# A graph network on one core: where the rows of the first attention layer are multiplied

## The reference

```python
def sage_layer(h, Ws, Wn, b):                      # network 1, three times
    agg = jax.ops.segment_sum(h[src], dst, num_segments=N) / deg
    return jax.nn.relu(h @ Ws + agg @ Wn + b)

def gat_conv(x, src, dst, W, att_src, att_dst, bias, heads, C, concat):   # network 2, twice
    h = (x @ W).reshape(n, heads, C)
    a_src = jnp.einsum('nhc,hc->nh', h, att_src)
    a_dst = jnp.einsum('nhc,hc->nh', h, att_dst)
    e = jax.nn.leaky_relu(a_src[src] + a_dst[dst], NEG_SLOPE)
    ...                                            # softmax of e over the edges of one dst: alpha
    out = jax.ops.segment_sum(h[src] * alpha[:, :, None], dst, num_segments=n)
    return out.reshape(n, heads * C) + bias
```

## Time and profile before

| | |
|---|---|
| time, median of 3 runs | 7210.41 us (7204.28 to 7210.7) |
| profiled execution, its own time | 7209.73 us |
| its span | 7207.8 us, mean PE clock 0.801 of full |
| PE busy | 5032.8 us (70%) |
| DVE busy | 4784.7 us (66%) |
| ACT busy | 3062.6 us (42%) |
| POOL busy | 3388.1 us (47%) |
| DMA | 1317.61 MB, mean 183 GB/s |

### The profile page before, as it was taken

One profiled execution on the slowest core, in us unless ns is written; L12 is line 12 of the kernel. 1 busy time (PEld: TensorE's weight loads), 2 busy tenths in 40 slices (PEclk: granted clock), 3 DMA queues, 4 the chain that ended last, 5 costly groups with the idle time before them and its releaser, 6 DMA issues. The chain is left out here.

```text
span 7207.8 us, 88239 instructions
## 1 busy us (share of the span) xinstructions
PE 5032.8 (70%) x24324; PEld 3367.5 (47%) x24324; DVE 4784.7 (66%) x14503; ACT 3062.6 (42%) x6979; POOL 3388.1 (47%) x3407
## 2 busy tenths in 40 slices
PE   7999995798989920697435555444489998679221
PEld 5777771364558810596323232221156665456111
DVE  5888789733347612888885566677878886655454
ACT  4666660263333300654444444336756554346000
POOL 5666000274434454373567666673300001765677
PEclk9999999999998955597557667665589999889555
DMA  5888551496766621696445698757856665766332
GB/s 194 277 276 277 214 198 61 126 305 226 245 205 203 195 67 35 175 350 212 140 137 148 129 136 131 122 100 219 270 197 222 222 223 199 209 203 194 95 93 82
DMA packets 1093011, 1317.61 MB, mean 183 GB/s; under 512 B 110351, under 2 KB 791999, under 8 KB 1086254
## 3 DMA queue, kind: packets, MB, share of 16 engines
q1 hardware_dynamic: 974926, 1058.13, 44.3%
q0 software_dynamic: 117600, 253.84, 17.3%
HBM read 633.42 MB, written 682.00 MB: 183 GB/s over the span
## 5 line engine op out<-in xcount | busy, mean ns | idle before, releaser
L615 POOL DMA_INDIRECT jk_layer_msg<-jk,idx_jk x588 | 591.5, 1006 | 268.2 <-issue 174.0
L615 POOL DMA_INDIRECT gcn_msg<-x,idx x196 | 186.9, 954 | 898.0 <-POOLq L137 838.6
L1148 PE MATMUL jk_layer_sum_ps<-ident,jk_layer_weighted 128*128 128x128 f32 x784 | 185.5, 380 | 540.5 <-ACT jk_layer_weighted L1114 540.5
L1148 PEld LDWEIGHTS jk_layer_sum_ps<-ident,jk_layer_weighted 128*128 128x128 f32 x784 | 118.6, 188 | 660.2 <-ACT jk_layer_weighted L1114 660.2
L742 PE MATMUL gcn_nodes_h_ps<-gcn_nodes_h_t,w_gcn 128*128 128x512 f32 x784 | 352.7, 593 | 0.0
L742 PE MATMUL sage_nodes_h_ps<-sage_nodes_h_t,w_ws 128*128 128x512 f32 x784 | 352.5, 592 | 0.0
L1282 DVE COPY sage_h<-sage_turn 128x512 f32<-128x512 f32 x98 | 67.7, 691 | 417.3 <-PE sage_turn L733 417.3
L615 POOL DMA_INDIRECT sage_small_rows<-meta,src_node x196 | 185.0, 944 | 324.2 <-POOLq L137 264.8
L962 ACT ACTIVATE sage_nodes_h_t<-sage_nodes_h_ps,w_b_c 128x512 f32<-128x512 f32 x392 | 247.8, 683 | 198.8 <-PE sage_nodes_h_ps L742 198.8
L2185 PE MATMUL gcn_end_sum_ps<-ident,gcn_end_rows 128*128 128x128 f32 x196 | 54.6, 434 | 389.4 <-DVE gcn_end_rows L2178 389.4
L615 POOL DMA_INDIRECT sage_end_msg<-h,idx x196 | 197.0, 1005 | 270.2 <-ACT sage_end_weighted L1114 159.5
(11 more groups left out here) (481 smaller groups left out, 15979.2 us busy)
## 6 DMA issues: line engine op xcount, KB each, us to landing
h<-sage_nodes_h SPq DMA_DIRECT2D x196, 512.0 KB
h_t<-sage_h_t SPq DMA_DIRECT2D x98, 512.0 KB
h<-sage_h SPq DMA_DIRECT2D x98, 512.0 KB, 3.6
jk_t<-jk_layer_h_t SPq DMA_DIRECT2D x196, 256.0 KB
jk_end_layers<-jk_t SPq DMA_DIRECT2D x49, 1024.0 KB, 5.3
r<-gcn_nodes_h SPq DMA_DIRECT2D x98, 512.0 KB
second_x_in<-u SPq DMA_DIRECT2D x147, 260.0 KB
jk<-jk_layer_h SPq DMA_DIRECT2D x147, 256.0 KB, 4.5
```

The costliest lines, as they stand in the source:

```text
L615: pool.indirect_dma_start(out=into[:, g.number % depth, s, :], out_offset=None, in_=table, in_offset=bass.IndirectOffsetOnAxis(ap=index_ti ...
L1148: mm = pe.transpose(ps[:, c, at_s], self.weighted[:, g.b, s, c * P:(c + 1) * P], self.K.ident[:])
```

## The change

The product of the first attention layer moves. For slots it was made at the end of `sage_end_block` and stored, and the fetch gathered its rows. Now `sage_end_block` ends with the norm and stores x1 only, and the fetch is replaced by `products_block("products1")`, the former second product made general: per round it takes one group of edges, whose rows of **x1** POOL gathers, and one group of slots, whose rows of x1 SP loads, and turns, copies and multiplies both. Edge results go to `kept`, slot results to `u`, scores beside them. For edges whose source is a node without edges, x1 must be in memory too, so `node_net_block` stores it: one more store of 256 KB per group on SP's queue, placed between the stores of h2 and u, and one more wait of DVE. In `sage_end_block` the own rows and the inputs get three buffers and the product two banks, and the product takes the own rows first. Nobody gathers scores any more, so `u` has 128 columns instead of 130 everywhere, and `attend_block` and the second product use rows of 512 bytes. The second product is otherwise the same code under new names.

```diff
-        x1_t, u = ph.sb("x1_t", [P, 2, 1, GROUP]), ph.sb("u", [P, 2, SUB, D + 2])
+        x1_t, u = ph.sb("x1_t", [P, 2, 1, GROUP]), ph.sb("u", rows4)
         x2 = ph.sb("x2", rows4)
         x1_turned, x1_copied, u_made, u_out, z_summed = (S(n) for n in ("x1_turned", "x1_copied", "u_made", "u_out", "z_summed"))
-        u_stored = ph.dma_sems("u_stored")
+        u_stored, x1_stored = ph.dma_sems("u_stored"), ph.dma_sems("x1_stored")
...
+        def store_x1(g):
+            wait_for(sp, norm.done, g)
+            sp.dma_start(at(node_rows(tables["x1"], SLOTS), g), z[:, g.b]).then_inc(x1_stored.of(g), 16)
+
         def store_u(g):
             wait_for(sp, u_biased, g)
             sp.dma_start(at(node_rows(tables["u"], SLOTS), g), u[:, g.b]).then_inc(u_stored.of(g), 16)
         if sage:
-            stages = [(load, -1), (reload, 3), (store_h1, 3), (store_h2, 4), (store_u, 7), (store_y, 6)]
+            stages = [(load, -1), (reload, 3), (store_h1, 3), (store_h2, 4), (store_x1, 5), (store_u, 7), (store_y, 6)]
         else:
             stages = [(load, -1), (reload, 4), (store_x3, 2), (store_h1, 4), (store_h2, 5), (store_y, 6)]
         run_groups(sp, NG, stages)
-        for stored in (h1_stored, h2_stored, y_stored) + ((u_stored,) if sage else (x3_stored,)):
+        for stored in (h1_stored, h2_stored, y_stored) + ((u_stored, x1_stored) if sage else (x3_stored,)):
...
-            layer_rows(pe, ring[:, :, 0:D + 2], [(W.wide["gat1"][:, :, 0:D + 2], x1_t[:, g.b])]).then_inc(u_made.sem, 1)
+            layer_rows(pe, ring[:, :, 0:D], [(W.m["gat1"], x1_t[:, g.b])]).then_inc(u_made.sem, 1)
...
                 wait_for(dve, x1_turned, g.lag(2))
+                wait_for(dve, x1_stored, g.lag(2))
...
-    own_t, own_ready = ph.sb("own_t", [P, 2, 2, GROUP]), A_("own_ready")
-    x1_t, u = ph.sb("x1_t", [P, 2, 1, GROUP]), ph.sb("u", [P, 2, SUB, D + 4])
-    x1_ps, u_ps = ph.ps("x1_ps", [P, GROUP]), ph.ps("u_ps", [P, SUB, HID])
-    x1_turned, x1_copied, u_made, u_out, att_out = (S(n) for n in ("x1_turned", "x1_copied", "u_made", "u_out", "att_out"))
-    u_stored = A_("u_stored")
-    x_in, y, z = (ph.sb(n, rows4) for n in ("x_in", "y", "z"))
-    y_ps = ph.ps("y_ps", [P, GROUP])
+    own_t, own_ready = ph.sb("own_t", [P, 3, 2, GROUP]), A_("own_ready", 1, 3)
+    x_in, y, z = ph.sb("x_in", [P, 3, SUB, D]), ph.sb("y", rows4), ph.sb("z", rows4)
+    y_ps = [ph.ps(f"y_ps{b}", [P, GROUP]) for b in range(2)]
     norm = Norm(ph, "norm")
-    x_loaded, z_stored = A_("x_loaded"), A_("z_stored")
+    x_loaded, z_stored = A_("x_loaded", 1, 3), A_("z_stored")
     made, biased, added = S("made"), S("biased"), S("added")
     block = ph.block()
 
     @block.sync
     def _(sp):
         def load_own(g):
-            wait_for(sp, made, g.lag(2))
-            sp.dma_start(own_t[:, g.b], at(tables["h2_t"], g)).then_inc(own_ready.of(g), 16)
+            wait_for(sp, made, g.lag(3))
+            sp.dma_start(own_t[:, g.number % 3], at(tables["h2_t"], g)).then_inc(own_ready.of(g), 16)
 
         def load_x(g):
-            wait_for(sp, added, g.lag(2))
-            sp.dma_start(x_in[:, g.b], at(slot_rows(tables["x_own"]), g)).then_inc(x_loaded.of(g), 16)
+            wait_for(sp, added, g.lag(3))
+            sp.dma_start(x_in[:, g.number % 3], at(slot_rows(tables["x_own"]), g)).then_inc(x_loaded.of(g), 16)
 
         def store_x1(g):
             wait_for(sp, norm.done, g)
             sp.dma_start(at(slot_rows(tables["x1"]), g), z[:, g.b]).then_inc(z_stored.of(g), 16)
-
-        def store_u(g):
-            wait_for(sp, u_out, g)
-            sp.dma_start(at(slot_rows(tables["u"]), g), u[:, g.b, :, 0:D + 2]).then_inc(u_stored.of(g), 16)
-        run_groups(sp, EG, [(load_own, 0), (load_x, 0), (store_x1, 3), (store_u, 4)])
-        for stored in (z_stored, u_stored):
-            wait_for_all(sp, stored)
+        run_groups(sp, EG, [(load_own, -1), (load_x, 0), (store_x1, 3)])
+        wait_for_all(sp, z_stored)
...
     def _(pe):
         def make(g):
+            wait_for(pe, own_ready, g)
+            wait_for(pe, biased, g.lag(2))
             wait_for(pe, sums.carried, g)
-            wait_for(pe, biased, g.lag(1))
-            wait_for(pe, own_ready, g)
-            layer_rows(pe, lanes(y_ps, D), [(W.m["wn2"], sums.sum_t[:, g.b]), (W.m["ws2"], own_t[:, g.b])]).then_inc(made.sem, 1)
-
-        def turn_x1(g):
-            wait_for(pe, norm.done, g)
-            wait_for(pe, x1_copied, g.lag(1))
-            turn_rows(pe, x1_ps, z[:, g.b], K.ident).then_inc(x1_turned.sem, 1)
-
-        def make_u(g):
-            wait_for(pe, x1_copied, g)
-            wait_for(pe, u_out, g.lag(1))
-            for s in range(SUB):
-                pe.matmul(u_ps[:, s, 0:D + 4], x1_t[:, g.b, 0, s * P:(s + 1) * P], W.wide["gat1"][:, 0, :], start=True, stop=False)
-                mm = pe.matmul(u_ps[:, s, 0:D + 4], K.ones[0:1, :], W.gat1_wide_b[:], start=False, stop=True)
-            mm.then_inc(u_made.sem, 1)
-        run_groups(pe, EG, [(lambda g: sums.tensor_sum(pe, g), 0), (make_u, 3), (make, 1), (turn_x1, 2)])
+            layer_rows(pe, lanes(y_ps[g.b], D), [(W.m["ws2"], own_t[:, g.number % 3]), (W.m["wn2"], sums.sum_t[:, g.b])]).then_inc(made.sem, 1)
+        run_groups(pe, EG, [(lambda g: sums.tensor_sum(pe, g), 0), (make, 1)])
 
     @block.scalar
     def _(act):
-        def copy_x1(g):
-            wait_for(act, x1_turned, g)
-            wait_for(act, u_made, g.lag(2))
-            act.copy(x1_t[:, g.b, 0, :], x1_ps[:]).then_inc(x1_copied.sem, 1)
-
-        def out_u(g):
-            wait_for(act, u_made, g)
-            wait_for(act, u_stored, g.lag(2))
-            wait_for(act, att_out, g.lag(2))
-            for half in range(2):
-                ins = act.copy(u[:, g.b, 2 * half:2 * half + 2, :], u_ps[:, 2 * half:2 * half + 2, 0:D + 4])
-            ins.then_inc(u_out.sem, 1)
-        run_groups(act, EG, [(out_u, 3), (lambda g: sums.scalar_weigh(act, g), -1), (copy_x1, 2), (lambda g: norm.scalar_root(act, g, W.eps), 1)])
+        run_groups(act, EG, [(lambda g: sums.scalar_weigh(act, g), -1), (lambda g: norm.scalar_root(act, g, W.eps), 1)])
 
     @block.vector
     def _(dve):
...
         def add(g):
             wait_for(dve, made, g)
             wait_for(dve, norm.done, g.lag(2))
-            dve.tensor_tensor(y[:, g.b], lanes(y_ps, D), to_subs(W.row["b2"]), ALU.add).then_inc(biased.sem, 1)
+            dve.tensor_tensor(y[:, g.b], lanes(y_ps[g.b], D), to_subs(W.row["b2"]), ALU.add).then_inc(biased.sem, 1)
             wait_for(dve, x_loaded, g)
             wait_for(dve, biased, g)
-            dve.scalar_tensor_tensor(y[:, g.b], y[:, g.b], 0.0, x_in[:, g.b], ALU.max, ALU.add).then_inc(added.sem, 1)
+            dve.scalar_tensor_tensor(y[:, g.b], y[:, g.b], 0.0, x_in[:, g.number % 3], ALU.max, ALU.add).then_inc(added.sem, 1)
             wait_for(dve, added, g)
             norm.vector_moments(dve, g, y)
 
         def apply(g):
-            wait_for(dve, x1_turned, g.lag(2))
             wait_for(dve, z_stored, g.lag(2))
             norm.vector_apply(dve, g, y, z)
-
-        def out_att(g):
-            wait_for(dve, u_out, g)
-            dve.tensor_copy(K.att[:, cols(g, SUB), :], u[:, g.b, :, D:D + 4]).then_inc(att_out.sem, 1)
-        run_groups(dve, EG, [(lambda g: sums.vector_carry(dve, g, [made]), 0), (out_att, 3), (apply, 2), (add, 1)])
+        run_groups(dve, EG, [(lambda g: sums.vector_carry(dve, g, [made]), 0), (apply, 2), (add, 1)])
...
-    heads, rows_wide = (2, D + 2) if first else (1, D)
+    heads = 2 if first else 1
...
+    own = ph.sb("own", [P, 3, SUB, D])
...
+def products_block(nc, name, K, W, tables, kept):
+
+    first = name == "products1"
+    ph = Phase(nc, name, 0)
+    kinds = ("edge", "slot") if first else ("edge", "node", "slot", "node")
...
+    wide_ps = {k: ph.ps(f"{k}_ps", [P, SUB, HID]) for k in ("edge", "slot")}
...
+    source, index = (tables["x1"], K.idx) if first else (tables["u"], K.idx_y)
+    weights, bias = (W.wide["gat1"], W.row["gat1_b"]) if first else (W.wide["gat2"], W.row["gat2_b"])
+    scores = 4 if first else 2
+    own_rows = slot_rows(source, 0 if first else V_ROWS)
+    result = slot_rows(tables["u"] if first else tables["yv"])
...
+            rows = at(own_rows, Group(r)) if kind == "slot" else at(node_rows(tables["u"], SLOTS), node_of(i))
+            sp.dma_start(x_in[:, n.number % 4], rows).then_inc(loaded.of(n), 16)
...
     def _(pool):
+        table = source[0:V_ROWS] if first else source
         for r in range(EG):
             g = Group(r)
             if r >= 4:
-                wait_for(pool, turned, Group(4 * (r - 4)))
+                wait_for(pool, turned, Group(per * (r - 4)))
             for s in range(SUB):
-                pool.indirect_dma_start(out=msg[:, r % 4, s, :], out_offset=None, in_=tables["u"],
```

(27 more changed lines are left out.)

138 lines of the change are left out of this document (51 added, 87 removed).

## The result

The changed kernel takes 7045.6 us (median of 4 runs, 7043.99 to 7049.17); the kernel before, measured beside it, 7207.34 (7197.51 to 7210.7). The ratio is 0.9778 (0.9762 to 0.9795): 162 us, where 137 were forecast. The profiled execution took 7044.68 us, span 7042.9, mean PE clock 0.819.

A forecast was written before the change was run, and what follows sets the result against it. PE was taken to bound the node network, last SAGE layer and second product, POOL the fetch. Terms -128.9 - 10.7 + 1 + 2 - 1 = -137.6 us gave a median of 7073 us, range 7056 to 7103.

The forecast's parts named there:

- loop of the last SAGE layer: Last SAGE layer's 48 groups: with PE's u work removed, they take 307.2 us, saving 128.9 us.
- 6.4 us a group: Last SAGE layer's period: DVE's chain of 6.24 us plus 0.16 for late products and waits; bounds 6.24 and 6.7.
- its tail: Last SAGE layer, last add to next stage's first gather: 9.25 us instead of 19.9, 10.7 saved.
- end of the first product: First product, after the last gather: POOL hides the rest, the exposed end costs +1 us, bounds -1 and +21.
- node network's store: Node network: the added stores of x1 cost 2 us through DMA share, bounds 0 and +7.
- narrower rows, second product: Second product: u rows of 512 instead of 520 bytes, still bound by PE; gain 1 us, bounds 0 and 3.
- a stage's saving is the program's saving: Whole kernel: stages follow one another behind barriers, so savings in changed stages sum to -137.6 us.
- without them PE could not run ahead: Last SAGE layer: third slots of own and x and second y bank let PE run ahead, giving 3.1 us slack.
- Rival A: Last SAGE layer: idle PE keeps its clock low, layer stays 436 us, only the tail saved, 7200 us; chance 0.08.
- Rival B: First product: bound by PE at the low clock, 5.4 us a round, +20 us, total 7093; chance 0.07.
- Rival C: Node network: transfers set its pace, so the added store makes the kernel slower, 1.55 us a group; chance 0.02.
- DVE is the next limit: Last SAGE layer: after the change DVE's chain of 6.24 us a group bounds it, DVE over 95% busy.

The follow-up runs named there:

- store_only: Kernel before plus x1 table placed as in the changed kernel, the node network's x1 store and DVE's wait for it: 7978.67 us, ratio 1.0009 to the kernel before.
- group 1: Runs on one chip: both kernels unchanged again, x1 table moved alone, store added; changed kernel 7855.76 us, ratio 0.9848 to the kernel before.
- group 3: Runs on one chip: kernel before twice, changed kernel, and changed kernel with seven gather buffers; changed kernel 7850.66 us, ratio 0.9864 to the kernel before.
- group 4: Runs on one chip: kernel before (7913.1 us), changed kernel (7808.93), and changed kernel without the first product's own-row loads (7787.74).
- group 2: Runs on one chip: kernel before (7902.93 us) and three kernels with edits around the last SAGE layer, ratios 0.9861, 0.9913 and 0.9884.
- b_look2: Kernel before, unchanged, profiled on the chip of group 2; last SAGE layer's loop 439.5 us, whole kernel 7902.93 us (7 runs).
- b_nobias: Kernel before without the one-row products that add the bias to u in the last SAGE layer: ratio 0.9913 to the kernel before, loop 360.9 us.
- twins: Two profiles of the kernel before, unchanged, in group 3: JK's first gather to last output rows 3722.0 and 3728.8 us.
- a_2buf: Changed kernel with the last SAGE layer's two slots, one y bank, load lag and product order as before: ratio 0.9861 to the kernel before, loop 302.1 us.
- a_zact: Changed kernel with the last SAGE layer's norm applied by ScalarE, DVE making only a small shift: ratio 0.9884 to the kernel before, loop 328.3 us.

## Why the prediction was wrong

By its own steps, with what the first pair of profiles shows:

| step | forecast | measured |
|---|---|---|
| loop of the last SAGE layer | -128.9 (6.4 us a group) | -136.8 (6.235) |
| its tail | -10.7 | -11.5 |
| end of the first product | +1 | +1.9 |
| node network's store | +2 | +1.3 here, not told from 0 by store_only |
| narrower rows, second product | -1 | about 0 |
| sum of the changed stages | -137.6 | -145 |
| all other stages | 0 | -20 |

**The step that failed in kind is a term that the sum does not have:** it says that "a stage's saving is the program's saving", holds the stages with unchanged code to be equal, and gives them no width in the range. With 145 us alone the profiled execution would have come to about 7065 us, inside the range. Of the 20 us more, most are in JK (12), GCN (3) and the last stage (3). In later pairs on one chip the stretch from JK's first gather to the last rows of the output differs, after less before, by +6.8 (group 1), 0 and -6.8 (group 3) and +13.9 us (group 4). In group 2 the three edited kernels differ from b_look2 by -0.6 to +3.5, and in JK alone by -0.9 to -9.9, b_nobias among them with -8.7, whose tables lie as before. A pair of twins differs by 6.8. So the code did not bring these 18 us again, and moving the table alone did not either. It is not shown that they are pure variation: the timed runs of the first chip have the 162 us too, before and after each within 13 us, and no later run was on a chip as fast. What places them there stays open. A width of 11 us for some 3,400 us of such stages would have held the result. The later pairs, from -6.8 to +13.9, span as much; the twins alone do not.

**The step that was mis-sized is the 6.4 us a group.** The row's sum, 5.03 + 1.21 = 6.24, is 0.03 us below the 6.27 of nearly every group; that it meets the mean of 6.235 to 0.01 is owed to the short last group. Most of the 0.16 on top, for late products, was not needed, and this mis-sizes the loop by 7.9 us. The reason given for the slots, that "without them PE could not run ahead", is wrong: in a_2buf the groups take the same 6.27 without them. The clock was feared to stay at 0.8 to 0.95 and was 0.99.

**What was right.** DVE is the next limit, busy 96%, and its add no longer waits. The tail by parts: 3.14, 1.35 and 4.71 us forecast; 3.10 from the add to the root's end (2420.10), 1.36 from the reciprocal (2420.20) to the store, 3.94 from there to the first gather. POOL paces the first product on the first chip, and what is exposed is its end.

**Rival A** (the clock stays low) is wrong: PE idles 26% of the stage and the clock is higher than before, 0.99 against 0.90. The Trainium skill (TensorE: Matmul & The Clock Gate, HAM oscillation) describes the fall of the clock on a kernel whose waits are longer than the bursts of matmuls between them. Here it is the other way round, at most 1.8 us of waiting in 6.27, so the rule was carried over to a case that it does not describe. In a_zact, where PE's pauses are irregular and reach 2.6 us, the mean is 0.89, in the rule's direction. **Rival B** is wrong on the first chip (1.8 us of waits of POOL for PE). On the other chips the first product costs some 38 us more, twice B's 20, by stops that B did not describe. **Rival C** is wrong there too (store_only).
